# Later first pass and later maxima in an attention and MoE kernel, with the chain into the expert phase and the second listing re-placed

## The chip, the cores and the metric

The kernel runs on one core of one Trainium2 chip. The metric is device time in microseconds (us) for one execution; the median of three runs counts. The engines are TensorE (PE in the profile, with PEld for its weight loads), VectorE (DVE), ScalarE (ACT), GpSimd (POOL) and SyncE (SP), which here does nothing but wait on semaphores and issue DMAs.

## The reference, cut to what matters

One post-norm transformer layer in f32: 8 batches of 1024 tokens, width 256, 16 heads of 16 with rotary positions, then two groups of 32 experts of which each token takes the best two.

```
q, k, v = x @ Wq.T + bq, x @ Wk.T + bk, x @ Wv.T + bv      # x is 8 x 1024 x 256
q, k    = rope(q), rope(k)                                 # 16 heads of 16
attn    = softmax(q @ k.T / 4)                             # per head, 1024 x 1024
x       = layernorm(x + (attn @ v) @ Wo.T + bo)
# x2 = x as 8192 x 256; for each of two groups of 32 experts:
w, e    = top_k(softmax(x2 @ router_w), 2)                 # sorted by expert
y       = (silu(xs @ wg[e]) * (xs @ wu[e])) @ wd[e] * w    # hidden width 128
out     = layernorm(x + (2 * sum(y of group 0) + 2 * sum(y of group 1)) / 4)
```

## The kernel before, in words

**Attention** is one long list of steps. A unit is four heads of one batch; it has STEPS = 16 steps (two query halves by eight key blocks), a batch has 4 units and so SPB = 64 steps, and the eight batches have 512 steps and 32 units. Two passes over the scores run at once on PE. The first pass (`score`, L931, into `ps_a`) computes the four matmuls of a step LEAD steps ahead; VectorE reduces them to row maxima (L1166, two instructions in a step). The second pass (`score_t`, L921, mostly into `ps_b`) computes the same scores transposed, with the maxima already taken off, because they stand as extra rows in `q_stack`; ScalarE takes the exponential (L795, four in a step) and `pv` (L949, 8 matmuls into `ps_o`) follows two steps later.

Between the passes lies the **maxima path** of a unit: `split_max` on VectorE, the job M (a transpose on PE, L880, and a copy on ScalarE, L784), and on SP `max_row` (L576), which sends four small DMAs from `max_rows` into the rows of `q_stack`. The first `score_t` of the unit waits for the semaphore `s_mrow` that these four count.

**What sets the order** is written by hand. `schedule` (L80) puts jobs at step numbers (M, the projections Q, K, V, the transposes T, the router products L, the count products R). `chain_at` (L107) gives the step numbers of the chain from a batch's attention output to its routing (output projection O, layer norm, T, L, top2, softmax, ranks, R, choices), and `list_at` (L121) those of its listing, in which POOL scatters token rows into one list per expert (L172, `rows_dram<-stage_sb`). `between` and `chores` do this for VectorE. Each engine works through its own list in order. On SP all transfers stand in one list, `turns`, sorted by step number and then by priority (a lower number first): `parts_out` (L542: the split features `parts_q_sb` and `parts_k_sb` of two units, 1 MB each, to DRAM) has priority 0, `stack` (L565: these back into `q_stack` and `k_stack`) 1, `max_row` 2, `stage_in` (L627: token rows for a listing, into one of two buffers of `stage_sb`, which waits until the scatters that used the buffer have ended) 7. In batches 2 to 6 the listing of the batch two before runs beside the attention; its scatters wait for `pv`.

**The hand-over.** The last batch has no own chain in this phase, only that of batch 6 (`nb - 2`), whose choices make the first expert lists complete enough to begin. The expert phase has slots of one tile (128 rows): 318 tiles, the second group's from tile NT = 159. For each tile PE does two transposes (L1678), the gate and up products (L1691), a transpose of the hidden tile (L1700) and the down product (L1713); ScalarE copies (L1601, L1607, L1613), POOL scatters the result (L1548, `place_y`), SP fetches the rows (L1451) 8 tiles ahead. The chain and the listing of batch 7 run beside the first tiles at slot numbers (L147 and L148: NORM_AT, O_AT, ... LIST_AT). `spread_inverse` (L495 to 502) sends the inverse softmax sums of batch 7 in 16 DMAs, 8 by SP and 8 by ScalarE in one go (L1622). In `weights()` (L1490) SP reloads the down weights of the second group, `w_d`, seven chunks of 512 KB.

Of the kernel before, what the change touches and what calls it, by code (L numbers as in the profile page):

```python
# [11 lines left out]
L, D, H, DH = 1024, 256, 16, 16  # L12
# [3 lines left out]
KC = L // P  # L16
UPB = H // G
STEPS = (L // HALF) * KC
SPB = UPB * STEPS
LEAD = STEPS + 6  # L20
NPART, NTERM = 2, 3


# [57 lines left out]
def schedule(nb):  # L81

    b_jobs, a_jobs = {}, {}
    put = lambda jobs, t, *job: jobs.setdefault(t, []).append(job)
    for b in range(nb):
        start, end = SPB * b, SPB * (b + 1)
        for u in range(UPB):
            put(b_jobs, start + STEPS * u - 4, "M", UPB * b + u)
        for c, at in enumerate((start - 56, start - 24)):
            for q in range(QUARTERS):  # L90
                put(b_jobs, at + q, "Q", b, c, q)
                put(b_jobs, at + QUARTERS + q, "K", b, c, q)
        for i in range(KC):
            put(b_jobs, start - 7 + i, "V", b, i)
        if b == nb - 1:
            continue
        at = chain_at(nb, b)
        for i in range(KC):
            put(a_jobs, at["O"] + i, "O", b, i)
        for i in range(KC // 2):  # L100
            put(b_jobs, at["T"] + i // at["rate"], "T", b, i)
            put(a_jobs, at["L"] + i // at["rate"], "L", b, i)
        put(a_jobs, at["R"], "R", b)
    put(a_jobs, chain_at(nb, nb - 2)["E"], "E")
    return b_jobs, a_jobs


def chain_at(nb, b):

    end = SPB * (b + 1)  # L110
    if b < nb - 2:
        at = dict(O=22, norm=23, scale=38, T=48, L=50, x1=48, top2=55, exp=67, route=68, choose=69, marks=72, R=76, ranks=77,
                  rank_sums=78, choices=82)
        rate = 1
    else:
        at = dict(O=22, norm=30, scale=40, T=42, L=43, x1=42, top2=45, exp=47, route=48, choose=48, marks=49, R=50, ranks=51,
                  rank_sums=52, choices=54, table=55, E=57)
        rate = 2
    return dict({name: end + t for name, t in at.items()}, rate=rate)


def list_at(nb, b, t):

    if b < nb - 3:
        return SPB * (b + 2) + (27 if t < KC - 2 else 38) + LISTS * t, 1
    if b == nb - 3:
        return SPB * (b + 2) + 23 + LISTS * t // 2, 2
    return SPB * (b + 1) + 56 + t, 2


BLANK = 4
# [12 lines left out]
NSP = 2 * NY  # L144


DEN_AT, NORM_AT, O_AT, SCALE_AT, T_AT, L_AT, TOP_AT, R_AT = 2, 8, 13, 24, 25, 29, 34, 42  # L147
OWNER_AT, LIST_AT, MARK_AT, STAGE_AT, W1_AT = (56, 66), (46, 84), 39, 31, 84  # L148
FIRST_AT, LAST_AT, ADD_LAG = 9, 7, 4
AHEAD = 8  # L150
NGU, HT_LAG, DOWN_LAG = 3, 2, 3
# [23 lines left out]
def program(nc, nb, dram, cols, width):  # L175
# [33 lines left out]
    with ExitStack() as ctx:  # L209
# [308 lines left out]
        def attention_sync(sp):  # L518
# [157 lines left out]
                        at, rate = list_at(nb, b, t)  # L676
                        turns.append((at - 1.5 * LISTS / rate, 7, stage_in, (b, t)))
            for u in range(n_units):
                turns.append((STEPS * u - 3, 2, max_row, (u,)))
                if u + 1 < n_units:  # L680
                    turns.append((STEPS * (u + 1) + 2, 3, o_out, (sp, u)))
            start = SPB * (nb - 1)
# [304 lines left out]
        def attention_vector(vec):  # L987
# [48 lines left out]
            def norm(b):  # L1036
                at = NORM_STEPS * b
                for i in range(KC):
                    vec.wait_ge(s_adrain, a_no[("O", b, i if chain_at(nb, b)["rate"] == 1 else KC - 1)] + 1)
                    vec.bn_stats(stats[:, i, :], y[:, i, :]).then_inc(s_norm, 1)  # L1040
                    yield 4
                vec.wait_ge(s_norm, at + KC)
                for i in range(KC):
                    vec.bn_aggr(mean_var[:, i, :], stats[:, i, :]).then_inc(s_norm, 1)
                    yield 1
                vec.wait_ge(s_norm, at + 2 * KC)
                yield from inverse_root(vec, s_norm, at + 2 * KC, mean_var[:, :, 1], rstd, half_var, newton)
                vec.wait_ge(s_norm, at + 2 * KC + 12)
                vec.scalar_tensor_tensor(shift[:, :], mean_var[:, :, 0], -1.0, rstd[:, :], ALU.mult, ALU.mult).then_inc(s_norm, 1)
                yield 1  # L1050
# [65 lines left out]
                                         keep["rank"][:, :, :, half], ALU.mult, ALU.add).then_inc(s_rank, 1)  # L1116
                yield 1

            chores = [(STEPS * u - 6, 0, split_max(u)) for u in range(n_units)]
            for b in range(nb):  # L1120
                for c in range(DC):
                    if b or c:
# [330 lines left out]
        def finish_sync(sp):  # L1453
# [36 lines left out]
            def weights():  # L1490
                for i, c in enumerate((0, 1, 4, 5, 6, 7, 2, 3)):
# [4 lines left out]
                    if c == 2:  # L1496
                        all_listed(sp, 3 * KC - NBK)
                    load_gate_up(sp, 1, c)
                yield NT + 1
                sp.wait_ge(s_down, NT)  # L1500
                for c in range(1, WCHUNK):
                    load_down(sp, 1, c)

            def combined():
# [39 lines left out]
        def finish_gpsimd(pool):  # L1544
# [18 lines left out]
            def listing():  # L1563
# [9 lines left out]
                    mark(m)  # L1573
                pool.wait_ge(s_remarked, 2 * KC)
                for m in range(KC, 2 * KC):
                    yield LIST_AT[0] + m - KC
                    if m == KC:
                        pool.wait_ge(s_rank, RANK_STEPS * (nb - 1) + LAST_RANK_STEPS)
                    scatter(m, 0)
                    scatter(m, 1)  # L1580
                for m in range(2 * KC, 3 * KC):
                    yield LIST_AT[1] + 4 * (m - 2 * KC)
# [9 lines left out]
        def finish_scalar(act):  # L1592
# [27 lines left out]
                                   ACT.Copy).then_inc(s_cdrain, 1)  # L1620

            def chain():  # L1622
                yield DEN_AT + 1
                spread_inverse(act, b, range(1, H, 2))
                for i in range(2):
                    yield SCALE_AT + i
                    act.wait_ge(s_norm, NORM_STEPS * nb)
# [545 lines left out]
```

## Time and profile before

| | us |
|---|---|
| runs | 2491.82, 2489.55, 2480.01 |
| median | 2489.55 |
| profiled execution, its own time | 2489.78 |
| its span | 2488.0 |
| mean granted clock of TensorE | 0.957 |
| PE busy | 2244.5 (90%) |
| VectorE busy | 1771.4 (71%) |
| ScalarE busy | 1612.8 (65%) |
| POOL busy | 1033.1 (42%) |

The profiled execution took 2489.78 us for a span of 2488.0; the 1.8 us around the span are taken as fixed. The span falls into four parts: a start in which the features of the first units are made (to about 112 us), the attention with both passes (to about 1660), the hand-over (to about 1745) and the expert tiles (to the end). A shorter time can only come from a stretch in which PE waits, runs at the lower clock, or does less beside other work; the share of busy time over the whole span doesn't tell which.

### The profile page before, as it was taken

What the parts mean: (1) busy time and instruction counts of PE and PEld (TensorE: products, weight loads), DVE (VectorE), ACT (ScalarE), POOL (GpSimd) and SP (SyncE); (2) the same over time, 40 slices, a digit from 0 to 9 for tenths busy, and PEclk for the clock granted to TensorE, in tenths of its full rate; (3) what the DMA queues carried; (4) which work ended last, traced back from release to release, by engine and by line L of the source; (5) the groups of instructions that cost most, each with busy time, mean ns of one, the idle gap of its engine ahead of it and who ended that gap; (6) DMA issues with size and microseconds to landing.
All of it is one profiled execution on the core that took longest, in us unless ns stands there. A gap on an engine that the chain in (4) does not pass through costs nothing.

```text
span 2488.0 us, 44339 instructions
## 1 busy us (share of the span) xinstructions
PE 2244.5 (90%) x12537; PEld 1131.1 (45%) x12537; DVE 1771.4 (71%) x3365; ACT 1612.8 (65%) x3612; POOL 1033.1 (42%) x886
## 2 busy tenths in 40 slices
PE   5999999998999999999999999987786989998884
PEld 3433333433433343343343333332664767776653
DVE  4888888889788888888978888862345323346766
ACT  1277777776876877777787687766353435555654
POOL 3121340343444355345344434434455565554442
PEclk6699999999999999999999999998898999999997
DMA  6223532444433643445444364544563565788886
GB/s 172 81 59 80 133 85 65 125 105 120 137 118 89 165 141 88 126 140 127 114 138 126 83 171 144 161 153 145 146 190 121 181 216 178 250 251 274 279 277 213
DMA packets 210346, 371.29 MB, mean 149 GB/s; under 512 B 32512, under 2 KB 150016, under 8 KB 205888
## 3 DMA queue, kind: packets, MB, share of 16 engines
q1 hardware_dynamic: 181784, 291.46, 42.6%
q0 software_dynamic: 27552, 75.40, 8.3%
q10 hardware_dynamic: 776, 1.59, 0.3%
q8 instruction: 112, 1.84, 0.3%
q14 instruction: 122, 1.00, 0.1%
HBM read 204.84 MB, written 135.69 MB: 137 GB/s over the span
## 4 chain that ended last, share of the span: by engine, by line
PE 68%; DVE 17%; DMA 4%; issue 4%; SPq 3%; ACT 2%; another core or an unknown queue 1%; POOL 1%; ACTq 0%; DVEq 0%; POOLq 0%
PE ps_a L931 21%; PE ps_o L949 16%; DVE maxima_sb L1166 11%; PE ps_a L1691 6%; PE ps_b L852 6%; PE ps_b L921 4%; PE ps_b L862 3%; PE ps_b L1713 3%; PE ps_b L1691 3%; PE ps_a L1678 2%; DMA back_sb<-y_dram 2%; PE ps_o L1713 1%; PE ps_b L1700 1%; DMA w_d_sb<-y_dram 1%; DVE w_gu_sb L2012 1%
## 5 line engine op out<-in xcount | busy, mean ns | idle before, releaser
L1166 DVE TENSOR_REDUCE maxima_sb<-ps_a 128x1 f32<-128x1024 f32 x1024 | 1228.4, 1219 | 237.4 <-PE ps_a L931 224.8
L795 ACT ACTIVATE probs_sb<-ps_b 128x512 f32<-128x512 f32 x2013 | 1077.5, 601 | 325.4 <-PE ps_b L921 310.9
L931 PE MATMUL ps_a<-k_stack_sb,q_stack_sb 48*128 48x512 f32 x2048 | 730.2, 454 | 77.0 <-DVE maxima_sb L1166 52.3
L921 PE MATMUL ps_b<-q_stack_sb,k_stack_sb 50*128 50x512 f32 x2013 | 753.7, 454 | 9.1 <-ACT probs_sb L795 8.4
L931 PEld LDWEIGHTS ps_a<-k_stack_sb,q_stack_sb 48*128 48x128 f32 x2048 | 310.5, 190 | 663.1 <-DVE maxima_sb L1166 353.1
L949 PE MATMUL ps_o<-probs_sb,v_sb_sb 128*32 128x512 f32 x4096 | 549.9, 609 | 1.1 <-ACT o_raw_sb L803 0.6
L1548 POOL DMA_INDIRECT y_dram<-y_rows_sb,spot_sb x318 | 310.6, 977 | 336.8 <-ACT y_rows_sb L1613 306.7
L921 PEld LDWEIGHTS ps_b<-q_stack_sb,k_stack_sb 50*128 50x128 f32 x2013 | 311.4, 185 | 82.1 <-ACT probs_sb L795 72.1
L172 POOL DMA_INDIRECT rows_dram<-stage_sb,listed_sb x208 | 201.1, 967 | 327.5 <-PE ps_o L949 304.3
L1691 PE MATMUL ps_a<-w_gu_sb,x_cols_sb 128*128 x848 | 239.3, 406 | 18.1 <-issue 8.4
L403 POOL TENSOR_TENSOR feat_qk_sb<-feat_qk_sb,trig_sb 128x1024 f32<-128x1024 f32 x30 | 71.3, 2375 | 302.6 <-DMA swapped_sb<-feat_qk_sb 291.6
L1691 PEld LDWEIGHTS ps_a<-w_gu_sb,x_cols_sb 128*128 128x128 f32 x848 | 149.7, 196 | 55.6 <-issue 39.7
L949 PEld LDWEIGHTS ps_o<-probs_sb,v_sb_sb 128*32 128x32 f32 x4096 | 80.7, 108 | 164.5 <-issue 58.9
L1607 ACT ACTIVATE gate_sb<-ps_a 128x128 f32<-128x128 f32 x212 | 58.9, 278 | 148.4 <-PE ps_a L1691 81.6
L1678 PE MATMUL ps_a<-consts_sb,x_rows_sb 128*128 128x128 f32 x636 | 125.2, 279 | 23.9 <-DMA x_rows_sb<-rows_dram 23.9
L1601 ACT ACTIVATE x_cols_sb<-ps_a 128x256 f32<-128x256 f32 x318 | 121.2, 381 | 34.2 <-PE ps_a L1678 32.1
L1986 DVE TENSOR_TENSOR spot_sb<-x_rows_sb,spare_sb 128x1 int32<-128x1 int32 x237 | 36.5, 154 | 149.8 <-issue 75.1
L1700 PE MATMUL ps_b<-consts_sb,hidden_sb 128*128 128x128 f32 x318 | 91.7, 288 | 54.7 <-DVE hidden_t_sb L1995 34.6
L1713 PE MATMUL ps_b<-w_d_sb,hidden_t_sb 128*128 x388 | 125.7, 407 | 3.5 <-ACT y_rows_sb L1613 3.5
L2012 DVE SCALAR_TENSOR_TENSOR w_gu_sb<-back_sb,weight_sb,w_gu_sb 128x256 f32<-128x256 f32 x160 | 77.7, 485 | 69.9 <-DMA back_sb<-y_dram 62.7
L1691 PE MATMUL ps_b<-w_gu_sb,x_cols_sb 128*128 x424 | 117.6, 401 | 4.5 <-ACT x_cols_sb L1601 1.6
L1678 PEld LDWEIGHTS ps_a<-consts_sb,x_rows_sb 128*128 128x128 f32 x636 | 91.5, 145 | 60.0 <-issue 18.6
(243 smaller groups left out, 2374.8 us busy)
## 6 DMA issues: line engine op xcount, KB each, us to landing
x_rows_sb<-rows_dram SPq DMA_DIRECT2D x318, 128.5 KB
back_sb<-y_dram SPq DMA_DIRECT2D x80, 256.0 KB
parts_dram<-parts_q_sb SPq DMA_DIRECT2D x16, 1024.0 KB
parts_dram<-parts_k_sb SPq DMA_DIRECT2D x16, 1024.0 KB
w_gu_sb<-w_gu SPq DMA_DIRECT2D x16, 1024.0 KB
swapped_sb<-feat_qk_sb SPq DMA_DIRECT2D x62, 256.0 KB
q_stack_sb<-parts_dram SPq DMA_DIRECT2D x62, 256.0 KB
k_stack_sb<-parts_dram SPq DMA_DIRECT2D x62, 256.0 KB
```

The source lines that it names most:

```text
L172: return pool.indirect_dma_start(dram["rows"][g], bass.IndirectOffsetOnAxis(ap=index, axis=0), source, None)
L795: act.activation(probs[t % NPR][:, j, :], src[:, :], ACT.Exp, scale=float(DH) ** -0.5).then_inc(s_bdrain, 1)
L852: ins = pe.matmul(out[:, 0:QUARTER], w[:, dc, c * P:(c + 1) * P], x_t[:, dc, q * QUARTER:(q + 1) * QUARTER], start=dc == 0, stop=dc == DC - 1)
L921: pe.matmul(out[:, :], k_stack[u % NSTK][lo:lo + XROWS, jj, kc * P:(kc + 1) * P].bitcast(F32R), q_stack[u % NSTK][lo:lo + XROWS, jj, qh * ...
L931: ins = pe.matmul(out[:, kh, :], q_stack[u % NSTK][lo:lo + ROWS, jj, qt * P:(qt + 1) * P].bitcast(F32R), k_stack[u % NSTK][lo:lo + ROWS, j ...
L949: ins = pe.matmul(ps_o[32 * j:32 * j + 32, :], v[:, at:at + 32], probs[t % NPR][:, j, :], start=kc == 0, stop=kc == KC - 1)
L1166: vec.tensor_reduce(maxima[u % 2][:, 1 - k, i:i + 1], src[:, :, :].rearrange("p a q -> p (a q)"), AX.X, ALU.max).then_inc(s_adrain, 1)
L1548: pool.indirect_dma_start(dram["y"][n // NT], bass.IndirectOffsetOnAxis(ap=spot[n % NSP][:, :], axis=0), y_rows[n % NY][:, :], None).then_ ...
L1601: act.activation(x_cols[n % NXT][:, :, :], ps_x[n % 2][:, 0:DC, :], ACT.Copy).then_inc(s_xc, 1)
L1678: ins = pe.transpose(ps_x[n % 2][:, dc, :], x_rows[n % NXG][:, dc * P:(dc + 1) * P], con("ident"))
L1691: ins = pe.matmul(ps_g[n % NGU][:, 0:2 * HID], x_cols[n % NXT][:, dc, :], w_gu[g][:, bass.ds(e * (DC * 2 * HID) + dc * 2 * HID, 2 * HID)], ...
L1713: pe.matmul(y_bank(n)[:, 0:D], hidden_t[n % 2][:, :], w_d[:, bass.ds(e * D + down_at(g), D)], start=True, stop=True).then_inc(s_down, 1)
```

## The change

- LEAD falls from 22 to 20 steps. `split_max` moves from 6 steps ahead of a unit to 4, the job M from 4 to 3, the turn of `max_row` on SP from 3 to 2.
- The chain of batches 0 to 5 has R, ranks and choices one step earlier. That of batch 6 begins its norm at step 23 behind the batch's end instead of 30, waiting for each eighth of the output projection by itself, and everything behind it comes two steps earlier; so does its listing.
- In the expert phase the chain of batch 7 comes two slots later. ScalarE sends its 8 inverse DMAs in four pairs, at slots 5 to 8, instead of all at slot 3. The second half of the listing of batch 7's first group has one scatter in a slot, from slot 51, instead of two in a slot from slot 46. The owner tables come two slots later.
- The seven loads of `w_d` for the second group stand in seven slots from 163 on instead of together at 160.

```diff
-LEAD = STEPS + 6
+LEAD = STEPS + 4
-            put(b_jobs, start + STEPS * u - 4, "M", UPB * b + u)
+            put(b_jobs, start + STEPS * u - 3, "M", UPB * b + u)
-        at = dict(O=22, norm=30, scale=40, T=42, L=43, x1=42, top2=45, exp=47, route=48, choose=48, marks=49, R=50, ranks=51,
+        at = dict(O=22, norm=23, scale=38, T=40, L=41, x1=40, top2=43, exp=45, route=46, choose=46, marks=47, R=48, ranks=49,
-    return SPB * (b + 1) + 56 + t, 2
+    return SPB * (b + 1) + 54 + t, 2
-OWNER_AT, LIST_AT, MARK_AT, STAGE_AT, W1_AT = (56, 66), (46, 84), 39, 31, 84
+OWNER_AT, LIST_AT, MARK_AT, STAGE_AT, W1_AT = (58, 68), (51, 84), 41, 33, 84
-                turns.append((STEPS * u - 3, 2, max_row, (u,)))
+                turns.append((STEPS * u - 2, 2, max_row, (u,)))
-                    vec.wait_ge(s_adrain, a_no[("O", b, i if chain_at(nb, b)["rate"] == 1 else KC - 1)] + 1)
+                    vec.wait_ge(s_adrain, a_no[("O", b, i)] + 1)
-            chores = [(STEPS * u - 6, 0, split_max(u)) for u in range(n_units)]
+            chores = [(STEPS * u - 4, 0, split_max(u)) for u in range(n_units)]
-                yield NT + 1
-                sp.wait_ge(s_down, NT)
                 for c in range(1, WCHUNK):
+                    yield NT + DOWN_LAG + c
+                    if c == 1:
+                        sp.wait_ge(s_down, NT)
                     load_down(sp, 1, c)
-                    yield LIST_AT[0] + m - KC
+                    yield LIST_AT[0] + 2 * (m - KC)
                     scatter(m, 0)
+                    yield LIST_AT[0] + 2 * (m - KC) + 1
                     scatter(m, 1)
-                yield DEN_AT + 1
-                spread_inverse(act, b, range(1, H, 2))
+                for i in range(4):
+                    yield DEN_AT + 3 + i
+                    spread_inverse(act, b, range(4 * i + 1, 4 * i + 4, 2))
```

On PE, at the very start of the program: the feature products of the first units (L852) and the first-pass steps between them.

```order
-L852 MATMUL ps_b<-x_t_sb,w_q_sb 128x256 x4
-L931 MATMUL ps_a<-k_stack_sb,q_stack_sb 128x512 x4
-L852 MATMUL ps_b<-x_t_sb,w_q_sb 128x256 x2
-L931 MATMUL ps_a<-k_stack_sb,q_stack_sb 128x512 x4
-L852 MATMUL ps_b<-x_t_sb,w_q_sb 128x256 x2
+L852 MATMUL ps_b<-x_t_sb,w_q_sb 128x256 x8
 L931 MATMUL ps_a<-k_stack_sb,q_stack_sb 128x512 x4
 L852 MATMUL ps_b<-x_t_sb,w_k_sb 128x256 x2
```

Two first-pass steps are gone from between the feature products, which now stand in one row.

On SP, the queue around the first step of a unit whose listing and whose `parts_out` fall together (unit 10 here; units 14, 18, 22 and 26 read alike).

```order
 L627 DMA stage_sb<-x_dram 128x2x256 x2
 L542 DMA parts_dram<-parts_q_sb 128x2x1024
-L576 DMA q_stack_sb<-max_rows_sb 1x16x128 x4
 L627 DMA stage_sb<-x_dram 128x2x256
 L542 DMA parts_dram<-parts_k_sb 128x2x1024
+L576 DMA q_stack_sb<-max_rows_sb 1x16x128 x4
 L565 DMA q_stack_sb<-parts_dram 16x2x1024
 L565 DMA q_stack_sb<-parts_dram 32x2x1024
```

The four sends of the maxima rows stood ahead of one `stage_in` and of the 1 MB of `parts_k`, and now stand behind both.

## Rows read from the trace of the kernel before

**Rows 1.** Stretches: us, busy PE PEld DVE ACT POOL, clock, DMA share, GB/s.

```profile
112.00:1660.00 1548.00, 1485.92 (x9048) 594.90 (x9046) 1323.95 (x1706) 1178.47 (x2288) 609.17 (x447) 1.00 0.45 120
1660.00:1745.00 85.00, 58.01 (x337) 21.15 (x337) 19.84 (x99) 55.19 (x110) 28.94 (x35) 0.82 0.38 121
```

**Rows 2.** PE in order of time: first-pass steps, then five later rows.

```profile
38.75 1.23 PE L931 MATMUL ps_a<-k_stack_sb,q_stack_sb 48*128 48x512 f32 x4 [19.75 <-DMA k_stack_sb<-parts_k_sb]
...
45.57 1.23 PE L931 MATMUL ps_a<-k_stack_sb,q_stack_sb 48*128 48x512 f32 x4
...
601.68 1.07 PE L949 MATMUL ps_o<-probs_sb,v_sb_sb 128*32 128x512 f32 x8
...
603.66 0.47 PE L921 MATMUL ps_b<-q_stack_sb,k_stack_sb 50*128 50x512 f32 x1
...
604.29 1.06 PE L949 MATMUL ps_o<-probs_sb,v_sb_sb 128*32 128x512 f32 x8
...
1698.62 1.06 PE L949 MATMUL ps_o<-probs_sb,v_sb_sb 128*32 128x512 f32 x8
...
1700.54 1.06 PE L949 MATMUL ps_o<-probs_sb,v_sb_sb 128*32 128x512 f32 x8
```

**Rows 3.** SP's queue around the first steps of units 10 and 18.

```profile
594.46 2.68 SPq L576 DMA_DIRECT2D q_stack_sb<-max_rows_sb  x4
602.99 0.37 SPq L627 DMA_DIRECT2D stage_sb<-x_dram  x1
603.45 0.41 SPq L542 DMA_DIRECT2D parts_dram<-parts_k_sb  x1
608.62 1.26 SPq L565 DMA_DIRECT2D q_stack_sb<-parts_dram  x3
...
1019.37 0.41 SPq L542 DMA_DIRECT2D parts_dram<-parts_k_sb  x1
1024.71 0.33 SPq L565 DMA_DIRECT2D q_stack_sb<-parts_dram  x1
```

**Rows 4.** PE in order of time at the end of the first pass.

```profile
1666.18 1.27 PE L921 MATMUL ps_b<-q_stack_sb,k_stack_sb 50*128 50x512 f32 x2 [6.12 <-ACT probs_sb L795]
```

**Rows 5.** ScalarE there, then PE at the count products and first tile.

```profile
1663.57 2.07 ACT L819 ACTIVATE y_sb<-y_sb,shift_sb,rstd_sb 128x256 f32<-128x256 f32 x4 [5.23 <-DVE shift_sb L1049]
...
1695.56 0.61 PE L905 MATMUL ps_a<-hot_sb,ones_bf_sb 128*128 128x512 bf16 x2
...
1744.86 0.66 PE L1678 MATMUL ps_a<-consts_sb,x_rows_sb 128*128 128x128 f32 x2 [15.58 <-DMA x_rows_sb<-rows_dram]
```

**Rows 6.** The inverse DMAs at tile 3: SP, ScalarE, PE.

```profile
1756.84 0.43 SPq L1472 DMA_DIRECT2D inv_dram<-den_sb  x1
...
1759.13 3.69 ACTq L501 DMA_DIRECT2D o_den_sb<-inv_dram  x8
1762.92 0.28 ACT L1607 ACTIVATE gate_sb<-ps_a 128x128 f32<-128x128 f32 x1 [8.83 <-DMA o_den_sb<-inv_dram]
...
1763.92 0.45 PE L1700 MATMUL ps_b<-consts_sb,hidden_sb 128*128 128x128 f32 x1 [7.31 <-DVE hidden_t_sb L1995]
```

**Rows 7.** Stretches, columns as above: the second listing, and undisturbed tiles.

```profile
1876.00:1942.00 66.00, 45.47 (x210) 33.88 (x209) 32.23 (x146) 20.64 (x66) 36.24 (x39) 0.90 0.37 121
...
2072.00:2129.00 57.00, 56.88 (x295) 45.52 (x294) 18.52 (x99) 30.55 (x98) 31.95 (x34) 1.00 0.57 182
```

**Rows 8.** POOL in order of time within that listing.

```profile
1898.95 0.96 POOL L172 DMA_INDIRECT rows_dram<-back_sb,listed_sb  x1 [0.30 <-issue]
1900.22 0.96 POOL L1548 DMA_INDIRECT y_dram<-y_rows_sb,spot_sb  x1 [0.30 <-issue]
```

**Rows 9.** The down-weight loads: SP, then PE in order of time.

```profile
2119.47 3.88 SPq L1397 DMA_DIRECT2D w_d_sb<-w_d  x7
...
2135.15 0.69 PE L1678 MATMUL ps_a<-consts_sb,x_rows_sb 128*128 128x128 f32 x2 [5.27 <-DMA x_rows_sb<-rows_dram]
2136.00 2.07 PE L1691 MATMUL ps_a<-w_gu_sb,x_cols_sb 128*128 x4 [0.16 <-issue]
```

More of the change, by code:

```diff
@@ L111, in chain_at @@
     if b < nb - 2:
-        at = dict(O=22, norm=23, scale=38, T=48, L=50, x1=48, top2=55, exp=67, route=68, choose=69, marks=72, R=76, ranks=77,
-                  rank_sums=78, choices=82)
+        at = dict(O=22, norm=23, scale=38, T=48, L=50, x1=48, top2=55, exp=67, route=68, choose=69, marks=72, R=75, ranks=76,
+                  rank_sums=77, choices=81)
         rate = 1
     else:
-        at = dict(O=22, norm=30, scale=40, T=42, L=43, x1=42, top2=45, exp=47, route=48, choose=48, marks=49, R=50, ranks=51,
-                  rank_sums=52, choices=54, table=55, E=57)
+        at = dict(O=22, norm=23, scale=38, T=40, L=41, x1=40, top2=43, exp=45, route=46, choose=46, marks=47, R=48, ranks=49,
+                  rank_sums=50, choices=52, table=53, E=55)
         rate = 2
@@ L144 @@
 NSP = 2 * NY
-DEN_AT, NORM_AT, O_AT, SCALE_AT, T_AT, L_AT, TOP_AT, R_AT = 2, 8, 13, 24, 25, 29, 34, 42
-OWNER_AT, LIST_AT, MARK_AT, STAGE_AT, W1_AT = (56, 66), (46, 84), 39, 31, 84
+DEN_AT, NORM_AT, O_AT, SCALE_AT, T_AT, L_AT, TOP_AT, R_AT = 2, 10, 15, 26, 27, 31, 36, 44
+OWNER_AT, LIST_AT, MARK_AT, STAGE_AT, W1_AT = (58, 68), (51, 84), 41, 33, 84
 FIRST_AT, LAST_AT, ADD_LAG = 9, 7, 4
```

## The prediction

> **What bounds the kernel now.** I read the busy time by stretch first. Through the attention PE is busy 1486 of 1548 us at full clock, in the hand-over 58 of 85 at 0.82 [rows 1]. So in the attention every step counts at its PE time, and a wait of PE is lost whole; in the hand-over and the expert tiles time lies in the gaps. Then I read PE in order of time and took the pitch between `pv` groups. A step in which both passes run takes 604.29 − 601.68 = 2.61 us, one with the second pass alone 1700.54 − 1698.62 = 1.92 [rows 2]. Then I read what ended each large gap, and for each moved transfer the SP queue around the point to which it moves.
>
> **First pass, start.** The first `score` waits for `k_stack` and starts at 38.75; that stays. Before, the stretch to 45.57 holds two first-pass steps and the feature products that now stand ahead of the first step, inside that wait [rows 2]. So 6.82 us go at the start. The total of steps is the same, so two of them change kind: at the end two steps of the second pass alone become dual, 2 × (2.61 − 1.92) = +1.4 if nothing waits. Net −5.4.
>
> **End of the first pass.** Here the exponentials wait behind the norm's four activations, which waited for VectorE's `shift_sb`; PE stood 6.12 us [rows 4] behind ScalarE's wait of 5.23 [rows 5]. The norm now starts seven steps earlier, so that wait goes. Behind the gap PE ran at half clock for some 8 us (clock 0.82 in the hand-over, rows 1), which I price at 3 to 4. Gained 6.1 + 3.9 = 10, less 1.7 for what is late next: in the two steps of the eight scale activations, 4 × 0.52 us stand beside four exponentials (4 × 0.417) in a step of 2.61, which is 1.1 too much in each, partly buffered. Together 8.3. The maxima path of the last unit is shorter by one step of 1.92 and gets 3.9 us for some 5.4: +1.5. Hence −5.4 − 8.3 + 1.5 = −12.2. By dependence I get more. The count product R stood at 1695.56 and the first tile at 1744.86 [rows 5], 49.3 us that VectorE, POOL and the landings set and that the change doesn't shorten. R moves from step 50 to 48 behind batch 6, and the T and L products, which came after the last first-pass step, now fall into dual steps, so those two steps (2 × 1.92 and the 0.4 of their PE work) come off the path ahead of it: −4.3. I take −12.2 − 4.3 = −16.5; by itself, with the steps to R not counted, −12.2, is its upper end, and −20 with no overload and a free last unit its lower. +1 for the 1 MB load of the residual, which now stands between two `stage_in` loads.
>
> **Maxima sends behind the listing.** This is the term that decides. In units 10, 14, 18, 22 and 26 the sends stood ahead of a `stage_in` and of `parts_k`; now they stand behind both. Before, unit 10's sends went out from 594.46 for 2.68 us, nine us ahead of the unit's first `score_t` at 603.66 [rows 2, 3]. `stage_in` waits for scatters that wait for the batch's own `pv`, so it can't come sooner: it issued at 602.99, `parts_k` at 603.45 [rows 3]. The sends would begin at 603.9, the fourth by 605.7 (0.6 each, a quarter of the 2.68 less the first wait). Landing takes at least the 2.2 us that the inverse took from its issue at 1756.84 to the reads that waited for it at 1759.13 [rows 6], so `s_mrow` comes no sooner than 607.95, 4.3 after the first `score_t`. The 1 MB of `parts_k` landed at 608.62, when the reads that wait for it issue, 5.2 after its issue (unit 18: 1024.71 − 1019.37 = 5.3) [rows 3]. If the small sends come behind it, the wait is 5.0. I take 5.0. Behind such a wait the clock falls: after a gap of 5.27 us the four L1691 products took 2.07 us, against 1.03 two tiles on [rows 9], and after the 6.12 the clock was also low; a shorter gap may leave it. I price this at 1.5, so 6.5 a unit, 32.5 for five. From both sides: 4.3 without loss of clock is 21.5 in all; 5.5 + 3 is 42. Nothing else can fill the wait, because the first-pass matmuls stand behind the waiting `score_t` on PE; VectorE and ScalarE then wait for PE and give nothing back, since PE is what bounds. In the other units with `parts_out` the order also turns, but `parts_k` is ready early and the path had 8 to 12 us of room; one step less (2.61) leaves room. Only unit 2 is near: +0.3.
>
> Why 5.0 and not 4.3: the Trainium skill, page "DMA: Bandwidth & Descriptors", section "Queues, rings and completion order", says that a semaphore's increment is a write that lands only after every earlier write of the same DMA engine. By that rule the sends count as landed only behind `parts_k`, at 608.6; the row of `parts_k` shows its own landing, and no row here shows a small send behind it. Without the rule the sum would be 3.5 lower.
>
> **Tile 3.** ScalarE issues eight DMAs in 3.69 us behind a wait, and its next activation comes 8.83 late; PE stands 7.31 [rows 6]. Now four pairs lie at slots 5 to 8, when the inverse has landed. Three tiles there took 9.1, 3.4 and 2.9 us against 1.7 undisturbed, 10.4 lost. Left are 4 × 0.93 us of issues, of which I count 1.4, and 1.5 of waiting for the residual. Gain 7.5, from 4 to 10.
>
> **Second listing.** In the stretch of 66 us PE is busy 45.5 at a clock of 0.90; undisturbed it is busy 56.9 of 57 with 34 tiles, 1.68 a tile [rows 7]. So 20.5 us are idle, and up to 6.6 go to the clock. POOL works there without a break, 1.27 us for each indirect DMA [rows 8], three to a tile: 3.8 against 1.68, over eight tiles 17 us. Two to a tile is 2.53, over sixteen tiles 13.6. That alone gives 3.4. The other 10 are lumps and clock; of these I take a little over half, as no gap of several us is left to drop the clock. Gain 9, from 0 to 18.
>
> **Down-weight loads.** Seven loads of 512 KB issued in a row in 3.88 us hold up `x_rows`, PE waits 5.27 and then runs slow [rows 9]. One in each slot of 1.7 us is 300 GB/s beside the rows' own traffic, close to what the chip moves here, so a little stays. The tile's pitch is 8.7 against 1.6. Gain 6.5, from 4 to 7.5.
>
> The earlier R of batches 0 to 5 has one answer: nothing near waits for it. 0.
>
> **Sum.** −16.5 + 1 + 32.5 + 0.3 − 7.5 − 9 − 6.5 = −5.7. The profiled execution took 2489.8 and lies 0.2 over the median, which I leave: 2484.
>
> **Rivals.**
> *The sends cost more and the gaps stay* (slower). The price of a unit is 5 + 3 = 8 us when the clock falls for as long as behind the 6.12 gap, +7.5; and the gaps of the expert phase move rather than go (gains 4, 0 and 4 instead of 23), +15. It gives 2507. For it: POOL must place the same number of scatters, SP the same bytes. Against: the gaps at tile 3 and at the loads come from a burst, and bursts are what goes. It decides, at 2502, from a price of 10.1 a unit (6.5 + 18.2 / 5), or of 8 with gains under 12.3. Chance 0.13.
> *The clock holds* (faster). Waits of 4.4 without a fall are 22 instead of 32.5, and the listing gives 14 instead of 9: 2484 − 10.5 − 5 = 2469. For it: 4.4 is under the shortest gap (5.27) behind which rows here show a fall. Against: the five gaps are close to it. Chance 0.25.
> *The sends are not late.* If `stage_in` is let through earlier, since the scatters ahead of it end earlier, the five waits shrink to nothing: 2484 − 32.5 = 2452. The order of SP speaks against it, and the release by `pv`, which moves with the unit. Chance 0.05.
> *The expert gaps only move.* As in the first rival, without its clock: 2484 + 15 = 2499. Chance 0.12.
> My forecast, 2484, has 0.45.
>
> **How the numbers follow.** A difference under 0.5%, 12.4 us, is about what a measurement of this kernel can't tell from none, so the bounds are 2477 and 2502. The forecast's own range is 2477 to 2492. Faster: 0.25 + 0.05 = 0.30. Within: 0.45 + 0.12 = 0.57. Slower: 0.13. The range leaves out the case of 2452 and the upper half of the slower one: 2463 to 2504, from 0.05 below and about 0.08 above, and the ends of the unknown terms beyond it make up the rest of the 2 in 10.
>
> **What would show it.** In the changed kernel's trace: the first `score_t` of units 10, 14, 18, 22 and 26 behind a gap of 4 to 5.5 us released by the sends into `q_stack`; the granted clock below 1 in slices behind them; no gap of 6 us before the transposes of batch 6's `y_sb`, and the first tile at 1744.9 − 16.5 + 1 + 32.5 + 0.3 = 1762; eight activations at tile 3 without a wait over 3 us; POOL with a break between its pairs or not; no 5 us gap seven tiles into group two. The forecast is wrong if the five gaps are absent, if they last over 8 us, or if a new gap stands where the listing is now denser with the loads of the second group.

## The result

The changed kernel takes 2524.3 us (2517.1 to 2532.3) against 2489.5, 35 us more by the medians: ratio 1.0148, 95% interval 1.0107 to 1.0189. Once more on another chip it was 1.0181 (1.0152 to 1.0210). The forecast was 2484, 6 us faster, in a range of 2463 to 2504. The profiled execution took 2521.8 us with a span of 2520.0, 32.0 more than that of before.

The page's rows of the second pass on PE and of the maxima on VectorE; the columns are busy us, mean ns, idle us ahead of them and what ended it:

```profile
L1166 DVE TENSOR_REDUCE maxima_sb<-ps_a 128x1 f32<-128x1024 f32 x1024 | 1228.1, 1219 | 286.1 <-PE ps_a L931 274.8
L921 PE MATMUL ps_b<-q_stack_sb,k_stack_sb 50*128 50x512 f32 x2017 | 763.4, 459 | 32.7 <-DMA q_stack_sb<-max_rows_sb 29.2
```

The second pass had 9.1 us of idle time ahead of it before, and none on the sends; now 29.2 us end with them. By stretch (columns as in rows 1), the attention, hand-over and expert tiles:

```profile
104.00:1728.00 1624.00, 1522.65 (x9118) 611.60 (x9126) 1348.34 (x1723) 1190.50 (x2309) 609.16 (x447) 0.97 0.43 115
1728.00:1791.00 63.00, 43.85 (x267) 13.56 (x264) 16.83 (x86) 43.06 (x87) 28.92 (x35) 0.90 0.46 146
1791.00:2520.00 729.00, 618.16 (x2955) 465.94 (x2954) 356.79 (x1496) 363.64 (x1184) 364.43 (x382) 0.95 0.70 220
```

The attention, which ran at clock 1.00 [rows 1], is at 0.97 and longer. I took the start of the `pv` groups of both traces step by step, and of the tiles' first transposes, and read where their difference changes. Negative is earlier than before:

| where | forecast | measured |
|---|---|---|
| start, to the first `pv` | −6.8 | −8.9 |
| sends late, units 10, 14, 18, 22, 26 | +32.5 | +46.1 |
| M late, units 4, 8, ... 28 (seven) | 0 | +28.0 |
| units 9, 13, 17, 25, in the ranks' steps | 0 | −10.8 |
| end of the first pass, last unit, hand-over | −8.7 | −9.2 |
| small rests before the first tile | +0.3 | +0.6 |
| first tile | +17.3 | +45.8 |
| tile 3 (tiles 0 to 10) | −7.5 | −8.3 |
| second listing (tiles 48 to 80) | −9 | −4.4 |
| down weights (tiles 155 to 170) | −6.5 | −5.9 |
| rest of the tiles | 0 | +4.8 |
| sum | −5.7 | +32.0 |

The sends, SP's queue and PE in order of time at unit 10, where rows 2 and 3 stood:

```profile
595.42 0.36 SPq L627 DMA_DIRECT2D stage_sb<-x_dram  x1
596.22 0.36 SPq L542 DMA_DIRECT2D parts_dram<-parts_k_sb  x1
596.62 3.85 SPq L576 DMA_DIRECT2D q_stack_sb<-max_rows_sb  x4
600.87 1.74 SPq L565 DMA_DIRECT2D q_stack_sb<-parts_dram  x4
...
602.13 0.76 PE L921 MATMUL ps_b<-q_stack_sb,k_stack_sb 50*128 50x512 f32 x1 [5.65 <-DMA q_stack_sb<-max_rows_sb]
```

The order is the one forecast, and the wait is a little longer than the 5.0 forecast; PE's other four gaps there are 5.39, 7.07, 5.49 and 5.61 us. Behind them the clock is low for longer than forecast (busy time by stretch, columns as in rows 1, clock third from the end):

```profile
602.00:606.00 4.00, 3.87 (x15) 1.48 (x17) 1.22 (x1) 1.13 (x3) 0.50 (x1) 0.50 0.98 193
606.00:612.00 6.00, 6.00 (x30) 2.35 (x28) 4.10 (x10) 4.60 (x9) 1.41 (x2) 0.61 0.88 173
```

Together, idle time and low clock, the five places cost 9.4, 10.2, 9.2, 8.6 and 8.8 us.

The loss that was not forecast at all, at unit 20: POOL, VectorE and PE in order of time.

```profile
1133.52 4.55 POOL L720 TENSOR_TENSOR y_sb<-y_sb,bo_row_sb 128x2048 f32<-128x2048 f32 x1
...
1133.93 4.17 DVE L1020 TENSOR_SCALAR max_parts_sb<-maxima_sb 128x32 int32<-128x32 int32 x1
1138.14 0.19 DVE L1023 TENSOR_TENSOR max_parts_sb<-maxima_sb,max_parts_sb 128x32 f32<-128x32 f32 x1
...
1138.48 0.27 PE L880 MATMUL ps_b<-consts_sb,max_parts_sb 128*64 128x128 f32 x1 [2.47 <-DVE max_parts_sb L1023]
1139.85 0.79 PE L931 MATMUL ps_a<-k_stack_sb,q_stack_sb 48*128 48x512 f32 x1 [0.23 <-DVE maxima_sb L1166]
```

The first instruction of the split works on 128 x 32 values. It takes 0.16 to 0.55 us in 25 of the 32 units and 4.2 to 4.3 in units 4, 8, 12, 16, 20, 24 and 28, each time from 0.3 to 0.4 us behind the start of POOL's bias addition to its end. M then holds up PE for 2.46 us, and at unit 20 the matmul behind it takes 0.79 us instead of 0.50: half clock again. That isn't so each time. Behind the gaps of units 4 and 8 the clock stayed at 1.00, and the two places cost 2.0 and 2.3 us; behind the other five it fell, and they cost 3.6 to 6.9. The clock (third from the end) behind M of unit 8 and of unit 20:

```profile
485.70:490.00 4.30, 4.03 (x24) 1.99 (x25) 4.30 (x15) 2.44 (x6) 0.00 (x0) 1.00 0.03 8
1139.80:1146.00 6.20, 6.16 (x20) 2.38 (x20) 4.77 (x19) 2.41 (x5) 1.01 (x1) 0.50 0.10 29
```

In the kernel before the split stood two steps earlier and was over before POOL's addition began.

### The profile page after: what moved, and what is told of

Same layout as the page of the kernel before. It is cut to its first block, busy times and chain, and to the rows that moved or that the text cites. A ratio compares the mean times of both kernels' runs of the same rounds, so it can differ in the third digit from the quotient of the medians.

```text
span 2520.0 us, 44334 instructions
## 1 busy us (share of the span) xinstructions
PE 2259.8 (90%) x12529; PEld 1133.2 (45%) x12537; DVE 1787.2 (71%) x3365; ACT 1612.7 (64%) x3612; POOL 1036.8 (41%) x886
## 4 chain that ended last, share of the span: by engine, by line
PE 68%; DVE 16%; DMA 5%; issue 5%; SPq 2%; ACT 2%; another core or an unknown queue 1%; POOL 1%; ACTq 0%; DVEq 0%; POOLq 0%
PE ps_a L931 21%; PE ps_o L949 17%; DVE maxima_sb L1166 10%; PE ps_a L1694 6%; PE ps_b L852 5%; PE ps_b L921 4%; PE ps_b L1694 3%; PE ps_b L1716 3%; PE ps_b L862 2%; DMA back_sb<-y_dram 2%; PE ps_a L1681 2%; PE ps_o L1716 2%; PE ps_b L1703 1%; DVE max_parts_sb L1020 1%; DVE w_gu_sb L2015 1%
## 5 line engine op out<-in xcount | busy, mean ns | idle before, releaser
L921 PE MATMUL ps_b<-q_stack_sb,k_stack_sb 50*128 50x512 f32 x2017 | 763.4, 459 | 32.7 <-DMA q_stack_sb<-max_rows_sb 29.2
L931 PE MATMUL ps_a<-k_stack_sb,q_stack_sb 48*128 48x512 f32 x2048 | 739.9, 458 | 56.3 <-DVE maxima_sb L1166 46.0
L931 PEld LDWEIGHTS ps_a<-k_stack_sb,q_stack_sb 48*128 48x128 f32 x2048 | 316.8, 193 | 652.1 <-DVE maxima_sb L1166 358.7
L949 PE MATMUL ps_o<-probs_sb,v_sb_sb 128*32 128x512 f32 x4096 | 560.4, 620 | 1.2 <-ACT o_raw_sb L803 0.6
L921 PEld LDWEIGHTS ps_b<-q_stack_sb,k_stack_sb 50*128 50x128 f32 x2017 | 316.9, 188 | 107.6 <-ACT probs_sb L795 65.7
L1703 PE MATMUL ps_b<-consts_sb,hidden_sb 128*128 128x128 f32 x318 | 91.0, 286 | 48.1 <-DVE hidden_t_sb L1998 29.2
```

Source lines behind the costliest of these rows:

```text
L921: pe.matmul(out[:, :], k_stack[u % NSTK][lo:lo + XROWS, jj, kc * P:(kc + 1) * P].bitcast(F32R), q_stack[u % NSTK][lo:lo + XROWS, jj, qh * ...
L931: ins = pe.matmul(out[:, kh, :], q_stack[u % NSTK][lo:lo + ROWS, jj, qt * P:(qt + 1) * P].bitcast(F32R), k_stack[u % NSTK][lo:lo + ROWS, j ...
L949: ins = pe.matmul(ps_o[32 * j:32 * j + 32, :], v[:, at:at + 32], probs[t % NPR][:, j, :], start=kc == 0, stop=kc == KC - 1)
```

## The experiments

Each was timed beside the kernel before on the same chip, and each ratio compares such a pair. The first four ran on a chip that took 2426 us for the kernel before, the others on two chips that took 2481 and 2483. The changed kernel wasn't run on the chip of 2426, so what those four edits gain against it rests on ratios from different chips and on the traces.

**Sends three steps ahead again.**

```diff
-                turns.append((STEPS * u - 2, 2, max_row, (u,)))
+                turns.append((STEPS * u - 3, 2, max_row, (u,)))
```

> The changed kernel (2524 us) with one edit: SP's turn of the maxima sends back at 3 steps ahead of a unit, so that in units 10, 14, 18, 22 and 26 they stand ahead of the stage load and of parts_k again. Theory: the five waits of PE for the sends cost 9.1 us each from the idle time to the return of the full clock, 45 in all, and nothing else hangs on them: 2479, with the seven waits of the transposed maxima (2.46 us each, units 4, 8, ... 28) still there. Rival: PE's wait would come back as a wait for k_stack, since parts_k now goes out behind the sends: then under 20 us are gained, 2505 or more.

2421.4 against 2426.4 for the kernel before, ratio 0.9991 (0.9969 to 1.0013), where the 2479 expected is 0.996 of 2489. The five waits are gone, and at the five places this trace falls 8.6 to 10.2 us against that of the changed kernel: some 46 in all. The first tile comes at 1750.1 instead of 1790.7; the end of the first pass took some of it back. `k_stack` didn't become a wait. The seven waits of M stand as they were. SP's queue at unit 10:

```profile
593.30 2.69 SPq L576 DMA_DIRECT2D q_stack_sb<-max_rows_sb  x4
598.14 0.37 SPq L627 DMA_DIRECT2D stage_sb<-x_dram  x1
598.61 0.41 SPq L542 DMA_DIRECT2D parts_dram<-parts_k_sb  x1
```

**Split five steps ahead.**

```diff
-            chores = [(STEPS * u - 4, 0, split_max(u)) for u in range(n_units)]
+            chores = [(STEPS * u - 5, 0, split_max(u)) for u in range(n_units)]
```

> The changed kernel (2524 us) with one edit: split_max 5 steps ahead of a unit instead of 4, so that it starts before POOL's bias addition (4.5 us) and not 0.4 us behind its start. Theory: the first instruction of the split takes 4.17 us in units 4, 8, ... 28 because POOL holds something that both engines need; started before it takes 0.17 us, the seven waits of PE go, and with them about 28 us (17 idle, 11 of half clock): 2496. The five waits for the sends stay. Rival: VectorE is simply behind there, by its queue of reductions; then the split still ends late, PE still waits 1 us or more in those units, and under 10 us are gained: 2515 or more.

2457.6, ratio 1.0141 (1.0098 to 1.0183). The split takes 0.18 us in all seven units, and the waits of M are gone: 28 us at those places, as expected. But the first tile came only 9.3 us earlier, since the edit lost some 19 us elsewhere, 9 of them from unit 28 to unit 31, and the ratio is that of the changed kernel where 1.003 was expected. So the mechanism held, and the sum didn't.

**Both.**

> The changed kernel (2524 us) with both edits: sends 3 steps ahead, split 5 steps ahead. Theory: the two losses are independent and add up, 45 + 28: 2451, faster than the kernel before (2489) by 1.5%. No gap of PE over 1.5 us between 40 us and the end of the first pass. Rival: another wait of the same units comes up behind them (k_stack, or the maxima buffer), and less than two thirds of the 73 are gained: 2475 or more.

2403.6, ratio 0.9909 (0.9879 to 0.9939); the first tile at 1729.9. Of the 73 us expected some 60 came, by the ratios. Against the sends alone it is 20 us at the first tile, not 28: behind the places of M, batches 1 to 6 lose some 11 us, and the end of the attention gains some back. Part of the 11 is in VectorE, POOL and PE in order of time at unit 21:

```profile
1148.41 2.35 DVE L1020 TENSOR_SCALAR max_parts_sb<-maxima_sb 128x32 int32<-128x32 int32 x1
1150.80 0.19 DVE L1023 TENSOR_TENSOR max_parts_sb<-maxima_sb,max_parts_sb 128x32 f32<-128x32 f32 x1
...
1148.36 2.37 POOL L438 TENSOR_TENSOR o_feat_sb<-o_feat_sb,o_den_sb 128x1024 f32<-128x1024 f32 x1
...
1152.55 0.50 PE L931 MATMUL ps_a<-k_stack_sb,q_stack_sb 48*128 48x512 f32 x1 [1.85 <-DVE logits_sb L1010]
```

Five steps ahead, the split of a batch's second unit starts 0.05 us behind another POOL product and ends with it, and the counts of R, which stand in the same step, come late for PE.

**The listing's choices a step later again**, in batches 0 to 5.

```diff
-        at = dict(O=22, norm=23, scale=38, T=48, L=50, x1=48, top2=55, exp=67, route=68, choose=69, marks=72, R=75, ranks=76,
-                  rank_sums=77, choices=81)
+        at = dict(O=22, norm=23, scale=38, T=48, L=50, x1=48, top2=55, exp=67, route=68, choose=69, marks=72, R=76, ranks=77,
+                  rank_sums=78, choices=82)
```

> The changed kernel (2524 us) with one edit: in the chain of batches 0 to 5 R, ranks, rank sums and choices one step later again, as in the kernel before. Theory: the 10.8 us that the changed kernel gains in units 9, 13, 17 and 25 come from VectorE's listed_sb (0.18 us instead of 2.09), which no longer falls on POOL's first rotation product; one step later it falls on it again, and the gaps of 1.5 to 2 us in PE's first pass come back: 2534, listed_sb near 2 us in those units. Rival: they come from the first pass being 20 instead of 22 steps ahead; then nothing changes: 2524, listed_sb at 0.18.

2476.1 against 2426.4, ratio 1.0224 (1.0179 to 1.0268). The changed kernel didn't run on this chip, so the total doesn't settle it; the traces do, in part. In unit 17 the difference to the changed kernel rises by 3.1 us, in unit 21 by 3.5, with `listed_sb` at 2.10 and 2.22 us and gaps of PE of 1.89 and 1.97; in units 9, 13 and 25 it is 0.18 us long and nothing changes. VectorE and POOL at unit 17:

```profile
1002.76 2.10 DVE L1115 SCALAR_TENSOR_TENSOR listed_sb<-expert_sb,rank_sb 128x32 int32<-128x32 f32 x1
...
1002.45 2.38 POOL L403 TENSOR_TENSOR feat_qk_sb<-feat_qk_sb,trig_sb 128x1024 f32<-128x1024 f32 x1 [5.69 <-DMA swapped_sb<-feat_qk_sb]
```

In the kernel before it is 1.8 to 2.3 us long in four batches. In all ten traces with the earlier step it is 0.18 in every batch; in the two of the kernel before with one edit (below) it meets POOL's product in two batches each. So neither theory holds whole: the step avoids the meeting, but whether the old step runs into it depends on some tenths of a microsecond of when POOL's product starts, which other waits shift.

**The changed kernel again.**

> The changed kernel itself once more, beside others on one chip, since the kernel before took 2489 us where the changed one was first timed and 2426 where the first four edits ran. Its ratio to the kernel before is the base for the edits' own. If the five waits for the sends (45 us) and the seven for the split (28 us) are in it as before, and the gaps of the expert tiles are small on this chip, it is above the 1.015 of its first timing, since the gain of 14 us in the expert tiles is then smaller: about 1.02. If chips differ only by a factor, 1.015.

2526.0 against 2481.1, ratio 1.0181 (1.0152 to 1.0210), on a chip like the first. Its trace has the same five and seven waits of the same length, but the five places cost 52 us in it and the seven 34, against 46 and 28: the half clock lasted longer behind them. So the price of a gap isn't fixed, and the sums of one pair of traces are good to some 6 us each.

**The sends' turn alone**, in the kernel before.

```diff
-                turns.append((STEPS * u - 3, 2, max_row, (u,)))
+                turns.append((STEPS * u - 2, 2, max_row, (u,)))
```

> The kernel before with one part of the change alone: SP's turn of the maxima sends 2 steps ahead of a unit instead of 3 (M and the split stay 4 and 6 ahead). Theory: the order of the queue alone makes the loss, five waits of 5.4 to 7 us and 9 us each with the clock: 45 us slower, ratio 1.018. Rival: it takes the later split and M as well, since the rows are ready a step later in the changed kernel; then this part alone costs under 20 us, ratio under 1.008.

2533.1, ratio 1.0217 (1.0189 to 1.0244), 52 us slower, 7 more than expected. Its five gaps of PE are 5.46 to 5.94 us, and the five places cost 8.1 to 11.7 us each, 50 in all. Here M and the split are early, so the rows were ready long before; the place in SP's queue is enough.

```profile
596.99 3.87 SPq L576 DMA_DIRECT2D q_stack_sb<-max_rows_sb  x4
...
602.81 0.76 PE L921 MATMUL ps_b<-q_stack_sb,k_stack_sb 50*128 50x512 f32 x1 [5.94 <-DMA q_stack_sb<-max_rows_sb]
```

**Split and M alone**, in the kernel before.

```diff
-            put(b_jobs, start + STEPS * u - 4, "M", UPB * b + u)
+            put(b_jobs, start + STEPS * u - 3, "M", UPB * b + u)
-            chores = [(STEPS * u - 6, 0, split_max(u)) for u in range(n_units)]
+            chores = [(STEPS * u - 4, 0, split_max(u)) for u in range(n_units)]
```

> The kernel before with another part alone: split 4 and M 3 steps ahead of a unit (sends 3 ahead, first pass 22 ahead). POOL's bias addition starts 2.6 us behind a pv group in both kernels, so the split should fall on it here too. Theory: its first instruction takes 4.2 us in units 4, 8, ... 28, M waits, 28 us slower: ratio 1.011. Rival: the longer lead of the first pass gives the split room, so that no M waits over 1 us: ratio 1.00.

2513.7, ratio 1.0135 (1.0104 to 1.0166), 33 us slower, with the split at 4.2 to 4.3 us and PE's gap at 2.46 in the same seven units:

```profile
1128.02 0.27 PE L880 MATMUL ps_b<-consts_sb,max_parts_sb 128*64 128x128 f32 x1 [2.46 <-DVE max_parts_sb L1023]
```

**Split five steps ahead in a batch's first unit, four in the others, sends three.**

```diff
-            chores = [(STEPS * u - 4, 0, split_max(u)) for u in range(n_units)]
+            chores = [(STEPS * u - (4 if u % UPB else 5), 0, split_max(u)) for u in range(n_units)]
-                turns.append((STEPS * u - 2, 2, max_row, (u,)))
+                turns.append((STEPS * u - 3, 2, max_row, (u,)))
```

> The changed kernel with the sends 3 steps ahead and the split 5 steps ahead in the first unit of a batch only (4 in the others). With 5 in all units the split fell on POOL's product of the output features in the second unit of a batch, 0.5 to 2.4 us, and VectorE's logits or counts came late behind it, 1.5 to 2.8 us of PE in four batches. Theory: both collisions are avoided, some 8 to 10 us better than 2403.5 against 2426.4 before: ratio 0.987. Rival: those gaps are VectorE's load, not the lock: ratio 0.991 as with 5 in all.

2445.4 against 2481.1, ratio 0.9852 (0.9819 to 0.9884). One gap over 1.5 us is left between the first `score` and the end of the attention, and the attention runs at clock 1.00:

```profile
104.00:1660.00 1556.00, 1499.28 (x9150) 602.51 (x9148) 1326.73 (x1751) 1191.78 (x2316) 608.73 (x447) 1.00 0.45 121
```

It is 80 us under the changed kernel on the same chip. The two parts alone, 52 and 33, make 85 of slowing; what the rest of the change gains is then 85 − 45 = 40, and this version has 36 of it. That sum is rough: with each part alone two of the four meetings of `listed_sb` were gone as well, some 6 us, and these are among the gains too.

**POOL's bias addition later**, in the changed kernel.

```diff
-            pool_order.append((SPB * b + (57 if b < nb - 1 else SPB), "bias_y", (b,)))
+            pool_order.append((SPB * b + (62 if b < nb - 1 else SPB), "bias_y", (b,)))
```

> The changed kernel with one edit on POOL alone: its bias addition at step 62 of a batch instead of 57. VectorE's and PE's order is untouched. Theory: what holds up the split's first instruction is POOL's addition, so with that 5 steps later the split takes 0.2 us in units 4, 8, ... 28, no M waits 2.4 us, and the ratio falls by 0.011 from the changed kernel's 1.015 to 1.018, to about 1.005. Whatever VectorE issues beside the moved addition may be held up instead, by up to 4 us, which would take part of it back. Rival: the order of VectorE's own work makes the split late: then nothing changes, 1.016.

2500.8 against 2482.8, ratio 1.0078 (1.0048 to 1.0108), better than the changed kernel by 0.7 to 1.0%, on other chips. Five of the seven waits are gone; five sevenths of the 0.011 expected are 0.008. This run carries its own control. In batches 0 and 1 POOL has no listing between the two places, so its addition starts as before, and in units 4 and 8 the split takes 4.29 and 4.17 us. From batch 2 on the addition moves, and in units 12 to 28 the split takes 0.17. VectorE and POOL at units 4 and 20:

```profile
272.90 4.29 DVE L1020 TENSOR_SCALAR max_parts_sb<-maxima_sb 128x32 int32<-128x32 int32 x1
...
272.61 4.55 POOL L720 TENSOR_TENSOR y_sb<-y_sb,bo_row_sb 128x2048 f32<-128x2048 f32 x1
...
1132.18 0.17 DVE L1020 TENSOR_SCALAR max_parts_sb<-maxima_sb 128x32 int32<-128x32 int32 x1
...
1148.97 4.58 POOL L720 TENSOR_TENSOR y_sb<-y_sb,bo_row_sb 128x2048 f32<-128x2048 f32 x1
```

**The best version with a lead of 22.**

```diff
-LEAD = STEPS + 4
+LEAD = STEPS + 6
```

> The best version so far (sends 3 ahead, split 5 and 4 ahead, ratio 0.985) with the first pass 22 steps ahead again: what the shorter lead alone is worth. Theory: it took 9 us at the start (two first-pass steps at half clock) and gives 1.4 back as two more steps of both passes; what it did to the end of the first pass is the norm's, not its own. So 7 to 8 us slower than with 20, ratio 0.988, first pv 9 us later. Rival: with 22 the norm's four activations meet the steps without a first pass, which leaves ScalarE room, and a 6 us gap stays: then 12 us or more, 0.990.

2453.6 against 2482.8, ratio 0.9875 (0.9843 to 0.9907) beside 0.9852: about 6 us, but the two intervals overlap. In the traces the first `pv` comes 9.3 us later and the first tile 13.0, of which 3.6 are a wait for the last unit's sends; the tiles were 5 us shorter in this execution. No 6 us gap stands at the end of the first pass, though the two runs with the norm of before and the same lead have it (5.92 and 5.94 us), so it goes with the norm's place. The old norm with a lead of 20 wasn't run.

**The best version with the expert phase of before.** The slot numbers, the inverse DMAs, the scatters and the seven loads as in the lines with − of the diff above.

> The best version so far with all expert-phase edits undone (slots, inverse DMAs in one go, two scatters in a slot, seven loads in a row): their sum. By the stretches of the two first traces: inverse 8.3 us (tiles 0 to 10), listing 4.2 (tiles 48 to 80, where 9 was forecast), down weights 5.9 (tiles 155 to 170): 18 us slower, ratio 0.9925. Rival: as forecast, 23 us, 0.9945; or only 14 as the two totals from the first tile on differ, 0.991.

2460.0, ratio 0.9901 (0.9870 to 0.9932): 12 us, with an interval that holds all three guesses but the largest. The traces say more than the totals: tiles 0 to 10 26.3 against 18.9 us, 48 to 80 84.5 against 80.2, 155 to 170 31.9 against 27.7; 15.9 in all, near the 18 of the two first traces. But the other tiles were 6 us shorter here, and that is no effect of the edits: tiles 80 to 155 take 152.6 to 157.8 us in the five traces with the new tiles, and 152.7 to 154.9 in the four with the old, leaving out the chip of 2426. From the first tile on the five take 722 us on average and the four 739, so the expert-phase edits are worth some 17 us.

**The second listing over 21 slots.**

```diff
-                    yield LIST_AT[0] + 2 * (m - KC)
+                    yield LIST_AT[0] + 8 * (m - KC) // 3
-                    yield LIST_AT[0] + 2 * (m - KC) + 1
+                    yield LIST_AT[0] + (8 * (m - KC) + 4) // 3
```

> The best version so far with the sixteen scatters of the second listing spread over 21 slots (51 to 71) instead of 16. Theory: POOL is the bound in that stretch by 2.53 us a tile against 1.7 to 1.8 of PE; spread out it needs 7 transfers in 4 tiles, 2.2 a tile, so tiles 48 to 80 take 80 less 16 x 2.53 plus 21 x 2.2, which with the tiles it covers is 2 to 4 us less: ratio 0.984. Rival: the stretch is bound by stalls of ScalarE for a free y buffer, not by POOL's pace, and it changes nothing, or the lists come too late for tile 81 and it is slower.

2446.1, ratio 0.9843 (0.9812 to 0.9875); tiles 48 to 80 take 79.1 us, where they take 78.3 to 80.2 over 16 slots. No change that can be told.

## Why the prediction was wrong

The forecast missed by 38 us of the span: 28 from a term that wasn't in the sum (M), 14 from one that was too small (the sends, by their clock), less 11 from another that wasn't in it (the chain), and 7 from the rest.

**Start.** Right: −8.9 for −6.8. Over all traces the first `pv` stands at 101.5 to 108.5 us with the lead of 20 (ten) and at 109.3 to 114.3 with 22 (four), 7.3 apart on average.

**The sends.** The mechanism and the five units were right, and the wait nearly: 5.4 to 5.7 us of idle time and once 7.1, where 5.0 was taken in a range of 4.3 to 5.5. Of that, 1.2 us is the issue of the four sends, which took 3.85 us behind the 1 MB of `parts_k` and 2.68 alone. Whether they land only behind `parts_k` was not what decided, as I had it: `parts_k` was there at 600.87, the sends at 602.1. The rule of the Trainium skill that I weighed ("DMA: Bandwidth & Descriptors", "Queues, rings and completion order") is neither borne out nor against this. The term that was mis-sized is the clock, 1.5 us for about 3.4: of the ten us behind the gap eight or so ran at half clock. 9.2 for 6.5 a unit is 14 us of the miss, 4 by the wait and 9 by the clock. The rival in which the clock holds leaned on 5.27 us as the shortest gap with a fall behind it. The trace of before has shorter ones, as at unit 9 (PE, then the stretch behind it, clock third from the end):

```profile
567.50 0.50 PE L931 MATMUL ps_a<-k_stack_sb,q_stack_sb 48*128 48x512 f32 x1 [1.89 <-DVE maxima_sb L1166]
...
568.40:571.80 3.40, 3.40 (x14) 1.17 (x7) 1.95 (x3) 1.79 (x4) 2.54 (x2) 0.51 0.00 0
```

**M and the split.** This step failed. I took the later split and M together with the sends, as one path up to the first `score_t` with 8 to 12 us of room, and wrote "one step less (2.61) leaves room". The split itself moved by two steps against its unit. And two things are not on that path. M is a matmul in PE's own order, so PE waits for the split however early the rows are wanted. And the split's new place was never held against what POOL does at that time. By VectorE's own list it looked harmless: 0.17 us of work that at unit 20 began 2.1 us ahead of the time at which M could have run. That cost 28 us, and the runs in which the kernel before had it alone (33 us), and in which POOL's addition or the split moved away, show it. None of the signs that the prediction named looked at these units.

**The chain of batches 0 to 5.** "Nothing near waits for it. 0" failed in the same way with the other sign: −10.8. In the kernel before `listed_sb` met POOL's rotation product in four batches. One row of VectorE and one of POOL in the trace of before would have shown it:

```profile
980.02 2.15 DVE L1115 SCALAR_TENSOR_TENSOR listed_sb<-expert_sb,rank_sb 128x32 int32<-128x32 f32 x1
...
979.75 2.37 POOL L403 TENSOR_TENSOR feat_qk_sb<-feat_qk_sb,trig_sb 128x1024 f32<-128x1024 f32 x1 [5.23 <-DMA swapped_sb<-feat_qk_sb]
```

How much of the 10.8 is the step's own is open; the run that undid it lost 6.6 in two batches.

**End of the first pass and hand-over.** Right: −9.2 for −8.7, no gap over 1 us where the 6.12 stood, and the first tile's own wait is 13.7 us [rows 5: 15.6].

**The expert tiles.** By the pair of traces they gave 13.8 us of the 23 forecast, but 4.8 of that difference stand where nothing was changed; over all traces it is 17. Tile 3 and the loads were right (−8.3 and −5.9); at the loads the largest gap of PE is now this one:

```profile
2167.39 0.69 PE L1716 MATMUL ps_o<-w_d_sb,hidden_t_sb 128*128 x2 [0.91 <-DMA w_d_sb<-w_d]
```

The listing gave 4.4 of 9. POOL's pace alone gives the 3.4 that stood in the working; the other half, that lumps and clock would go, didn't come. POOL is at its pace for twice as many tiles, and ScalarE's results still come in bursts (POOL in order of time):

```profile
1936.66 0.96 POOL L1549 DMA_INDIRECT y_dram<-y_rows_sb,spot_sb  x1 [0.34 <-issue]
1937.93 0.96 POOL L172 DMA_INDIRECT rows_dram<-back_sb,listed_sb  x1 [0.31 <-issue]
1941.02 0.96 POOL L1549 DMA_INDIRECT y_dram<-y_rows_sb,spot_sb  x1 [2.13 <-ACT y_rows_sb L1615]
```

**The rivals.** The slower one had the right place and sign for 14 of the 38 us. By its own terms it would not have decided: the price of a unit was over its 8 us but under 10.1, and the gains of the tiles were over 12.3. No rival held M. The range didn't allow for a term that the sum had at nothing.

## What to carry to other kernels

When an instruction is moved, hold its new time against what the other engines do then, not only against its inputs and its reader: a 0.17 us VectorE instruction can last as long as the POOL instruction that it meets. A row whose mean is far over that of its like, or that ends exactly with an instruction of another engine, is the sign. In a queue, a small urgent transfer belongs ahead of one that waits for something else; its turn cost nothing here when early and 8 to 12 us when late, since a gap of 5 to 6 us in a PE that was hardly ever idle was paid nearly twice, with the clock.

## What the runs showed of the hardware

- An instruction of POOL can hold up one of VectorE until it ends, and the wait shows as a longer VectorE instruction, not as idle time. The split's first instruction (128 x 32, int32, SBUF to SBUF) took 4.17 us against a POOL addition of 4.55 that had started 0.4 us earlier, 2.35 against a product of 2.37, and 0.17 free; `listed_sb` 2.1 against 2.4. The row maxima (reading PSUM) that ran beside the same additions in the version with both edits kept their 1.2 us. The Trainium skill states this ("SBUF — State Buffer", "SBUF: two separate sides"): the port pair that the two engines share is an exclusive lock for a whole instruction, not a division of bandwidth, against a VectorE instruction in a two-port mode or with two inputs in SBUF. The traces agree as to the lock: in all these meetings VectorE's instruction ends 0.03 to 0.05 us behind POOL's. In which mode the split's first instruction ran, no row shows.
- With one POOL instruction it was not so for its whole length. Beside POOL's L440 (2.85 us, a bias for each partition) the changed kernel's split ended with it in three units and long before it in two (0.33 and 0.49 us). Over all traces a split that began up to 0.84 us into it ended 1.14 to 1.15 us into it, one that began 1.1 to 1.7 us into it took its free 0.16 to 0.18 us, and one that began 1.83 to 2.69 us into it ended with it. Why is open.
- The four sends of 8 KB took 2.45 to 2.68 us to issue alone (kernel before, the five units) and 3.71 to 4.44 behind a transfer of 1 MB.
- The granted clock fell to 0.50 at gaps of 5.4 us and more each time, in the changed kernel for 10 to 17 us. At its seven gaps of 2.46 us it fell in five, for 3.4 to 10.2 us, and stayed at 1.00 in two; unit 4 lost 2.0 us in all, unit 20 6.9. In the kernel before it fell at gaps of 1.89, 1.95 and 2.10 us and not at one of 1.55. What makes the difference is open.
- The same kernel before took 2426 us on one chip and 2481 to 2489 on the others. In the versions traced there the attention was no shorter; the expert tiles took 673 to 676 us where the changed kernel's took 729 and 723. There POOL's transfers followed each other through the second listing with 0.3 us between them, where on the others some waited 2 us. Why is open.
